# A selective scan and a quantised feed-forward block on one core: part of the squares moved from ScalarE to VectorE, and a new order for all engines

## What is computed

```python
# state-space layer, per batch; d_inner = 256, 16 states
x = silu(conv(in_proj(ctx)) + conv_b)
dt_low, B, C = split(x_proj(x)); dt = softplus(dt_proj(dt_low) + dt_b)
state = state * exp(dt * A) + (dt * u) * B      # a scan over the 256 tokens
y = (sum over states of state * C + D * x) * silu(z)
x_tokens = x_tokens + tanh(g) * y
# feed-forward block, hidden = 704
xq = quant(layernorm(x_tokens)); x1, x3 = split(xq @ w13.T)
gated = square(relu(x1)) * x3
iq = quant(rmsnorm(gated, norm_w)); out = iq @ w2.T
x_tokens = x_tokens + tanh(g2) * out
```

## Time and profile before

| | us |
|---|---|
| median of three runs | 161.22 |
| the profiled execution's own time | 163.65 |
| its span in the profile | 161.8 |
| TensorE busy | 150.4 |
| ScalarE busy | 142.3 |
| VectorE busy | 122.9 |
| GpSimdE busy | 122.4 |

### The profile page before, as it was taken

The page is one execution under the profiler, slowest core; times in us unless marked ns, Lnnn a source line. Parts: engine busy times, 40 slices in busy tenths (PEclk is TensorE's granted clock), DMA queues, the critical chain, the costliest instruction groups (busy, mean ns, idle before and its releaser), DMA issues.

```text
span 161.8 us, 3705 instructions
## 1 busy us (share of the span) xinstructions
PE 150.4 (93%) x1298; PEld 119.3 (74%) x1298; DVE 122.9 (76%) x158; ACT 142.3 (88%) x361; POOL 122.4 (76%) x117
## 2 busy tenths in 40 slices
...
GB/s 112 375 358 243 113 254 329 17 78 242 222 39 40 2 54 223 232 221 61 4 2 169 249 215 203 208 4 0 2 36 0 2 36 0 32 0 4 34 65 65
DMA packets 26500, 18.39 MB, mean 114 GB/s; under 512 B 13481, under 2 KB 21106, under 8 KB 26354
## 3 DMA queue, kind: packets, MB, share of 16 engines
...
HBM read 15.94 MB, written 2.21 MB: 112 GB/s over the span
## 4 chain that ended last, share of the span: by engine, by line
ACT 43%; PE 29%; DMA 11%; issue 9%; DVE 4%; SPq 2%; POOL 1%; ACTq 0%; DVEq 0%; POOLq 0%
ACT dA L629 26%; PE w_ps L1013 8%; DMA b_diag<-low 5%; PE w_ps L997 5%; DMA bd<-b_diag 5%; PE m_ps L941 3%; PE w_ps L905 3%; PE w_ps L888 2%; ACT ru L691 2%; ACT duT L647 2%; DVE xc L752 2%; PE y_ps L872 2%; PE w_ps L897 2%; SPq L501 2%; DVE hb L799 1%
## 5 line engine op out<-in xcount | busy, mean ns | idle before, releaser
L799 DVE TENSOR_TENSOR_SCAN hb<-dA,m_ps 128x1024 f32<-128x1024 f32 x32 | 71.9, 2274 | 7.8 <-PE m_ps L941 4.7
L431 POOL TENSOR_TENSOR hb<-hb,cs 128x1024 f32<-128x1024 f32 x31 | 73.0, 2367 | 6.3 <-DVE hb L799 5.8
L629 ACT ACTIVATE dA<-dt,nega 128x255 f32<-128x255 f32 (+1 forms) x160 | 59.4, 454 | 0.0
L941 PE MATMUL m_ps<-bd,duT 64*128 64x128 f32 (+1 forms) x448 | 38.0, 311 | 2.9 <-DMA bd<-b_diag 1.3
L941 PEld LDWEIGHTS m_ps<-bd,duT 64*128 64x128 f32 x448 | 30.5, 197 | 9.8 <-issue 5.9
L967 PE MATMUL y_ps<-identf,hb 128*128 128x128 f32 x256 | 32.4, 275 | 0.2 <-DVE hb L431 0.2
L967 PEld LDWEIGHTS y_ps<-identf,hb 128*128 128x128 f32 x256 | 27.9, 140 | 2.6 <-issue 1.0
L997 PE MATMUL w_ps<-wT,xqT 128*128 128x352 bf16 x64 | 20.3, 318 | 0.5 <-ACT xqT L684 0.5
L997 PE MATMUL w_ps<-wres,xqT 128*128 128x352 bf16 x64 | 20.3, 317 | 0.0
L997 PE MATMUL w_ps<-wlo,xqT 128*128 128x352 bf16 x64 | 19.8, 310 | 0.0
L445 POOL TENSOR_TENSOR gw<-gg,normw 128x704 f32<-128x704 f32 x7 | 11.8, 1691 | 3.2 <-DVE gg L837 3.2
...
## 6 DMA issues: line engine op xcount, KB each, us to landing
...
```

The costliest lines, as they stand in the source:

```text
L431: E.tensor_tensor(h_g, h_g, cs[:, :, s0:s0 + sn, l0:l0 + ln], ALU.mult).then_inc(hc_end if (b, i, h) == OUT_END else hc_ok[h], 1)
L629: last = act_fn(dA_g[:, r, s, 1:ln], dt[:, b, h, l0 + 1:l0 + ln], ACT.Exp, scale=nega[:, h, at:at + 1])
L799: V.tensor_tensor_scan(hb[:, k % 3, h], decays, m_ps[:, h], 0.0, ALU.mult, ALU.add).then_inc(scan_ok[h], 1)
L941: last[r] = T.matmul(m_r[:, :, c * Q - l0:(c + 1) * Q - l0], duT[rows, p, h, (c - r) % CHUNKS, :], bd[rows, c, gs[0]:gs[-1] + 1].rearrange ...
```

## The change

In batches 2 and 3 ScalarE's step `relu` ends with the relu, and a new step `sq` on VectorE squares ru in place, one instruction for each of the eight 352-column parts. The step `gate` of these batches waits for the new semaphore sq_ok. Batches 0 and 1 are as before. 

```diff
+SQ_DVE = (2, 3)
...
-        ru_ok = sem("ru_ok")
+        ru_ok, sq_ok = sem("ru_ok"), sem("sq_ok")
...
                     act_fn(ru[:, h, c * UC:(c + 1) * UC], bank("up", b, i, 0)[:, 0:UC], ACT.Relu,
                            scale=finv[:, b, h:h + 1]).then_inc(free["act"], 1)
+                    if b in SQ_DVE:
+                        continue
...
+                elif name == "sq":
+                    h, c = i // 2, i % 2
+                    dve.wait_ge(free["act"], emptied("up", b, i, 0))
+                    r = ru[:, h, c * UC:(c + 1) * UC]
+                    V.tensor_tensor(r, r, r, ALU.mult).then_inc(sq_ok, 1)
...
                     dve.wait_ge(work_full, full("up", b, i, 1))
-                    dve.wait_ge(ru_ok, UPS * b + i + 1)
+                    if b in SQ_DVE:
+                        dve.wait_ge(sq_ok, UPS * SQ_DVE.index(b) + i + 1)
+                    else:
+                        dve.wait_ge(ru_ok, UPS * (b - sum(d in SQ_DVE for d in range(b))) + i + 1)
```

The table PLAN is new for all five engines: the same steps (and the eight `sq`) in another order. A piece of it, the end of TensorE's string (with the last sum, `sum1/3.3`) before and after:

```diff
-        sum0/3.3 xqT/3.0 iqT/1.1 sum1/3.3 down/1.0 up/3.0 up/3.1 xqT/3.1 up/3.2 up/3.3 iqT/2.0 down/1.1 iqT/2.1
-        down/2.0 down/2.1 iqT/3.0 iqT/3.1 down/3.0 down/3.1
...
+        up/2.2 sum1/3.3 up/2.3 xqT/3.0 up/3.0 iqT/1.1 down/1.0 xqT/3.1 up/3.1 up/3.2 up/3.3 iqT/2.0 down/1.1 iqT/2.1
+        down/2.0 iqT/3.0 down/2.1 iqT/3.1 down/3.0 down/3.1
```

More of the change, by code:

```diff
@@ L79 @@
[L79 to L83, removed]
@@ L84 @@
-        sum0/3.3 xqT/3.0 iqT/1.1 sum1/3.3 down/1.0 up/3.0 up/3.1 xqT/3.1 up/3.2 up/3.3 iqT/2.0 down/1.1 iqT/2.1
-        down/2.0 down/2.1 iqT/3.0 iqT/3.1 down/3.0 down/3.1
+        warm/0.3 bT/0.0 duT/0.0 warm/0.0 mix0/0.0 inproj/2.0 duT/0.1 mix1/0.0 inproj/3.0 mix0/0.1 warm/0.4 mix1/0.1
+        warm/0.5 mix1/0.2 mix0/0.2 skip/0.0 sum1/0.0 sum0/0.0 xdbl/2.0 xdbl/3.0 dtproj/1.0 dtproj/2.0 dtproj/3.0
+        mix0/0.3 szT/0.0 mix1/0.3 sum1/0.1 sum0/0.1 duT/1.0 duT/1.1 sum0/0.2 mix1/1.0 sum1/0.2 mix0/1.0 sum1/0.3
@@ new lines @@
+        sum0/0.3 mix1/1.1 duT/2.0 duT/2.1 skip/1.0 szT/1.0 mix0/1.1 sum1/1.0 sum0/1.0 mix1/1.2 xqT/0.0 mix0/1.2 up/0.0
+        szT/2.0 mix1/1.3 mix0/1.3 sum1/1.1 up/0.1 mix1/2.0 duT/3.0 mix0/2.0 sum0/1.1 sum1/1.2 mix1/2.1 sum1/1.3
+        sum0/1.2 sum0/1.3 mix0/2.1 duT/3.1 up/0.2 skip/2.0 mix1/2.2 mix0/2.2 up/0.3 sum1/2.0 mix1/2.3 sum0/2.0
+        mix0/2.3 sum1/2.1 sum1/2.2 xqT/1.0 sum0/2.1 mix1/3.0 mix0/3.0 sum1/2.3 sum0/2.2 sum0/2.3 mix1/3.1 up/1.0
+        mix0/3.1 up/1.1 skip/3.0 mix1/3.2 sum0/3.0 sum1/3.0 up/1.2 mix0/3.2 up/1.3 sum1/3.1 mix1/3.3 xqT/2.0 szT/3.0
@@ L86 @@
+        sum0/3.1 up/2.0 skip/3.1 mix0/3.3 iqT/0.0 iqT/0.1 sum1/3.2 sum0/3.2 up/2.1 down/0.0 down/0.1 iqT/1.0 sum0/3.3
+        up/2.2 sum1/3.3 up/2.3 xqT/3.0 up/3.0 iqT/1.1 down/1.0 xqT/3.1 up/3.1 up/3.2 up/3.3 iqT/2.0 down/1.1 iqT/2.1
+        down/2.0 iqT/3.0 down/2.1 iqT/3.1 down/3.0 down/3.1
     """,
     "act": """
-        tab/0.0 tap/0.0 tap/0.1 u/0.0 gates/0.0 u/0.1 tap/1.0 u/1.0 u/1.1 tab/0.1 soft/0.0 soft/0.1 tab/0.2 nega/0.0
-        duT/0.0 decay0/0.0 duT/0.1 decay1/0.0 decay0/0.1 xrs/0.0 decay1/0.1 tap/2.0 ud/0.0 decay0/0.2 tap/3.0
@@ L90 @@
[L90 to L99, removed]
@@ L100 @@
-        iqT/3.0 iqT/3.1
+        tab/0.0 gates/0.0 tap/0.0 tap/0.1 u/0.0 u/0.1 tap/1.0 u/1.0 u/1.1 tab/0.1 soft/0.0 soft/0.1 tab/0.2 nega/0.0
+        xrs/0.0 duT/0.0 decay0/0.0 decay1/0.0 duT/0.1 tap/2.0 decay0/0.1 decay1/0.1 tap/3.0 decay1/0.2 decay0/0.2
+        ud/0.0 decay0/0.3 decay1/0.3 tab/0.3 u/2.0 u/3.0 z/0.0 z/1.0 z/2.0 z/3.0 tab/0.4 soft/1.0 soft/2.0 soft/3.0
+        tab/0.5 decay1/1.0 szT/0.0 duT/1.0 duT/1.1 decay0/1.0 decay0/1.1 decay1/1.1 decay1/1.2 ud/1.0 decay0/1.2
+        xn/0.0 rs1/0.0 duT/2.0 ud/2.0 szT/1.0 quant1/0.0 duT/2.1 xqT/0.0 decay1/1.3 relu/0.0 decay0/1.3 szT/2.0
@@ new lines @@
+        decay0/2.0 decay1/2.0 relu/0.1 edge/3.0 duT/3.0 decay0/2.1 decay1/2.1 decay1/2.2 decay0/2.2 decay1/2.3
+        relu/0.2 square/0.0 duT/3.1 xn/1.0 decay0/2.3 rs1/1.0 decay1/3.0 relu/0.3 quant1/1.0 decay0/3.0 xqT/1.0
+        square/0.1 decay1/3.1 rs2/0.0 decay0/3.1 ud/3.0 relu/1.0 xn/2.0 decay1/3.2 relu/1.1 rs1/2.0 quant2/0.0
+        relu/1.2 decay0/3.2 relu/1.3 quant1/2.0 square/1.0 xqT/2.0 szT/3.0 square/1.1 quant2/0.1 relu/2.0 rs2/1.0
+        decay0/3.3 iqT/0.0 iqT/0.1 relu/2.1 decay1/3.3 quant2/1.0 rs1/3.0 xn/3.0 iqT/1.0 square/2.0 relu/2.2
```

45 lines of the change are left out of this document (22 added, 23 removed).

## The result

The changed kernel takes 167.7 us (median of 4 runs, 166.4 to 169.2) where the kernel before, beside it, took 162.2; the ratio is 1.031, with a 95% interval of 1.016 to 1.046. A second set on another occasion gave 165.9 against 161.5 us, 1.024 (1.015 to 1.033). So the change makes the kernel 2.4 to 3.1% slower. The medians are of all executions; the ratios leave out those over 1.5% above the fastest of the same kernel. The forecast was 160.9 us and its range ended at 164.8; it was wrong.

What follows compares the result with a forecast made beforehand. TensorE and ScalarE were taken as full up to the last scan, TensorE alone behind it. Start +1.6, middle -1.3 and -0.5, end -0.15 sum to -0.35 us; from the 161.22 us median that gives 160.9, range 157.4 to 164.8.

Steps and rivals of the forecast that it cites:

- The bound: Whole kernel: ScalarE and TensorE both full up to the last scan, TensorE alone behind it; chance 0.50.
- The price of the squares: Batches 2 and 3: each square costs VectorE 0.52 us, eight 4.2; ScalarE gets back 0.54 per pair, 4.3 in all.
- The start: Batch 0 up to dtproj: later table switch and one sum still to do cost TensorE +1.6 us.
- The middle: TensorE from 60 to 131.8 us: -1.3 for the bd wait and -0.5 for all other idle time.
- The wait for bd before batch 3: Before batch 3's first mix: bd group 1 lands earlier by the new queue order, so TensorE's wait goes, -1.3 us.
- I count it as gone: TensorE from 60 to 131.8 us: all idle time besides the bd wait vanishes, -0.5 us.
- The end: Behind the last sum: two old holes in TensorE's work close, new copy waits of 1.25 us open; net -0.15 us.
- Squares waiting for GpSimdE: Rival: VectorE's squares wait out GpSimdE's multiplies, 6.4 us lost, 3.2 come through, 163.9 us; chance 0.20.
- A start with more clock lost: Rival: TensorE's waits at the start make the clock fall some five us earlier, 163.9 us; chance 0.12.
- The fall that doesn't come: Rival: the clock fall from 39 to 46.5 us, costing 3.4 us, stays away, 157.5 us; chance 0.08.
- ScalarE as the bound: Rival: ScalarE alone bounds the kernel, so the 4.3 us taken off it come through, 156.9 us; chance 0.10.

Runs made afterwards that it cites:

- e11: e6 with the squares of batches 2 and 3 back on ScalarE, directly behind each relu; 163.2 us, 1.007 of the kernel before.
- e6: Changed kernel with engines and queue in the order of the kernel before up to the end of batch 0; 161.4 us, 0.997 of the kernel before.
- e10: Changed kernel with two queue edits: zeros behind the first c_rows put; old order from first cs transfer to bput/3.0. 162.3 us, 1.004 of before.
- e8: Kernel before with one queue change: bget/3.1 directly behind bget/3.0, cget/2.3 behind both; 161.9 us, 0.999 of the kernel before.
- e1: The changed kernel unaltered, measured again beside the kernel before; 165.9 us, 1.024 of the kernel before.
- e2: Kernel before in its own order, only the squares of batches 2 and 3 moved to VectorE ahead of their gates; 165.7 us, 1.028 of before.
- e9: Changed kernel with the 1 MB of zeros issued behind the first c_rows put; 164.1 us, 1.014 of the kernel before.
- e12: e6 plus 9 and 3 added identity transposes on TensorE ahead of xdbl/2.0 and xdbl/3.0; 160.7 us, 0.994 of the kernel before.

## Why the prediction was wrong, point by point

**The bound: right in the middle and at the end, not everywhere.** ScalarE was not the bound of the middle: e11, with all squares on ScalarE, has 0.7 us of TensorE's idle time there, and e6, with half of them moved, 0.8. But near 48 us TensorE isn't the bound either. In e6 the clock took 3.4 us from it between 39.3 and 46 us, and in e11 nothing up to there; still the mix that starts at 49.04 in e6 starts only 0.7 us earlier in e11 (48.33), since TensorE at full clock then waits 2.26 us for a scan.

**The price of the squares: right in size.** 0.49 to 0.53 us where 0.52 was worked out. ScalarE's busy time fell by 2.7 us only, not by 4.3 (by 3.1 from e11 to e6). In e6 six of the eight relus give way to the next instruction after 0.44 to 0.46 us, near the 0.43 of the prediction; behind the other two nothing follows at once, and their whole 0.55 us counts. That explains a part; the rest isn't shown.

**The start: here is the step that failed.** The forecast's +1.6 us took only the engines' order. The reordered queue of the start (x and the zeros ahead of weights, the first c_rows put behind them, the last 768 KB of weights late) stood in the sum at nothing, without a reason. Put right by the two edits of e10, it gives back 3.6 us of the median, and what it costs falls due behind 60 us. The part that was costed, the engines' order, is 0.9 us from e10 to e6 by the medians, and about 1.5 to 3 at the same clock; the 1.6 is neither confirmed nor refuted by that. That TensorE's idle time up to 60 us grew by 1.4, near the 1.6, proves nothing, since kernels with the same start differ by 1.2 in it.

**The middle: wrong.** -1.8 us was forecast and +1.2 came. The wait for bd before batch 3 went, as forecast, but that this saves 1.3 us isn't borne out: e8 alone is at 0.999 of before and saves some 0.2 us at the same clock (1.0 between the two profiles), since another wait grew behind it. And "I count it as gone" for all other idle time fails: the same kind of wait came up before batch 2 (1.27 us), by bget/1.3 late behind the last weights, bput/2.0 behind it, and bget/2.0 behind cget/1.3, cget/2.0 and normw. The prediction read this queue at one place, that of a wait that could be seen, and not at those where the old order had none. With the queue mended (e10), the middle has 0.8 us of idle time: -1.0 of the -1.8.

**The end: right.** -0.15 was forecast; TensorE's idle time behind the start of the last sum is 3.5 us before (26.07 less 22.53) and 3.4 in e1 (28.01 less 24.58). The last sum, forecast for 133.2, is at 134.4 in e1, and at 139.4 in the first profile with its lower clock (e1's last decay, last scan, its product and the last sum):

```profile
127.18 2.43 ACT L633 ACTIVATE dA<-dt,nega 128x127 f32<-128x127 f32 x8
```

```profile
130.12 2.29 DVE L805 TENSOR_TENSOR_SCAN hb<-dA,m_ps 128x1024 f32<-128x1024 f32 x1
...
132.69 1.22 DVE L435 TENSOR_TENSOR hb<-hb,cs 128x1024 f32<-128x1024 f32 x1
```

```profile
134.39 1.03 PE L981 MATMUL y_ps<-identf,hb 128*128 128x128 f32 x8
```

**The rivals.** Squares waiting for GpSimdE: the mechanism is real (squares of up to 1.26 us in e6 and 1.95 in e2), but it adds up to some 1.0 us in e1 and 1.7 in e2, and e6, with 1.5 us of it, is no slower than before. A start with more clock lost: the fall came a little later than before in e1, not earlier. In the first profile the clock lost 5.2 us of its span and before's 3.4, partly in a second fall:

```profile
102.00:104.00 2.00, 1.12 (x8) 1.12 (x9) 2.00 (x2) 1.97 (x9) 2.00 (x2) 0.86 0.84 242
104.00:106.00 2.00, 2.00 (x11) 2.00 (x10) 0.46 (x1) 2.00 (x8) 2.00 (x2) 0.50 0.37 119
```

That one comes in the stretch in which TensorE has work for only 1.12 of 2 us. How much of the first set's 5.5 us this is, the runs don't show. The fall that doesn't come: it came in e1 too, and its price of 3.4 us was too high. Beside e9 to e12 the kernel before has spans of 158.8 and 159.6 us at a clock of 1.00, and a median of 161.2 in its eight executions at 0.979: some 2 us. ScalarE as the bound would have given 156.9 us, and no run comes near it. The forecast's missing rival was a late transfer that takes the place of an early one.

What fits together: 165.9 us, less 3.6 by the two queue edits, less 0.9 by the engines' old start, gives 161.4. As ratios to the kernel before, whose own median differs from set to set, these are 1.024, 1.004 and 0.997. The first step is clear of the noise, the second is not. That the whole loss arises in the new start, queue and engines together, is shown by e6, whose interval reaches to 1.002 at most.
